# A state space block with a mixture of experts: ScalarE writes D times x into Y's bank and takes small pieces from VectorE

## The reference, cut to what matters

```
xb, z = split(rms_norm(x) @ in_proj_w)
xc    = silu(causal_conv(xb, 4 taps) + conv_b)
dt, B, C = split(xc @ x_proj_w);  dt = softplus(dt * dt_proj_w + dt_proj_b)
h_t   = exp(dt_t * A) * h_{t-1} + dt_t * B_t * xc_t      # per channel and state
y_t   = sum_states(h_t * C_t) + D * xc_t
out   = (y * silu(z)) @ out_proj_w + residual
```

## Time and profile before

| | |
|---|---|
| median of 3 runs | 2586.57 us (2585.44 to 2588.78) |
| profiled execution, its own time | 2586.42 us |
| its span in the trace | 2584.6 us |
| VectorE busy | 2375.5 us |
| TensorE busy | 2365.7 us |
| ScalarE busy | 1607.1 us |
| a steady pass (norms of pass 6 to norms of pass 7) | 967.91 to 1117.45: 149.5 us |

### The profile page before, as it was taken

The page is one execution under the profiler, slowest core; times in us unless marked ns, Lnnn a source line. Parts: engine busy times, 40 slices in busy tenths (PEclk is TensorE's granted clock), DMA queues, the critical chain, the costliest instruction groups (busy, mean ns, idle before and its releaser), DMA issues.

```text
span 2584.6 us, 26581 instructions
## 1 busy us (share of the span) xinstructions
PE 2365.7 (92%) x8416; PEld 1172.9 (45%) x8416; DVE 2375.5 (92%) x2821; ACT 1607.1 (62%) x3202; POOL 1495.0 (58%) x531
## 2 busy tenths in 40 slices
PE   5556899999999999999999999999999999988988
PEld 2112354544545454454545445454545545443554
DVE  3999999999999999999999999999999999999542
ACT  6566567675766666675766667666666756654231
POOL 0554566657565665666566666656666566666421
PEclk9768899999999999999999999999999999999999
DMA  4441433535353453535354353524444452543231
GB/s 154 163 147 69 144 130 124 177 98 186 113 160 120 139 168 103 180 117 166 110 157 150 104 179 118 184 95 156 149 126 159 122 183 84 166 133 96 72 76 57
DMA packets 172759, 344.48 MB, mean 133 GB/s; under 512 B 16043, under 2 KB 81356, under 8 KB 164172
## 3 DMA queue, kind: packets, MB, share of 16 engines
q1 hardware_dynamic: 164700, 334.93, 38.5%
q0 software_dynamic: 7920, 7.87, 2.3%
HBM read 291.35 MB, written 51.38 MB: 133 GB/s over the span
## 4 chain that ended last, share of the span: by engine, by line
DVE 63%; issue 18%; PE 10%; ACT 8%; DMA 1%; POOL 0%; DVEq 0%; SPq 0%; ACTq 0%; POOLq 0%
DVE hs L1051 29%; DVE hs L1037 14%; DVE th L1151 5%; DVE th L1146 5%; PE MY L503 2%; PE Gp L485 2%; PE Up L493 2%; DVE XC L1004 2%; ACT dA L592 1%; ACT SZ L665 1%; DVE SZ L1058 1%; ACT L592 1%; DVE DX L1026 1%; ACT L665 1%; PE FP L410 1%
## 5 line engine op out<-in xcount | busy, mean ns | idle before, releaser
L924 POOL TENSOR_TENSOR hs<-hs,Cb 128x2048 f32<-128x2048 f32 x256 | 1159.8, 4531 | 163.6 <-DVE hs L1037 163.6
L592 ACT ACTIVATE dA<-dtr,A 128x512 f32<-128x512 f32 x1024 | 700.7, 689 | 734.5 <-DVE hs L1051 732.2
L909 POOL TENSOR_TENSOR th<-th,cmb 128x512 f32<-128x512 f32 x256 | 326.3, 1278 | 906.2 <-DVE hs L1037 804.5
L1051 DVE TENSOR_TENSOR_SCAN hs<-dA,carry,hs 128x512 f32<-128x512 f32 x512 | 627.2, 1265 | 5.9 <-ACT dA L592 5.5
L1051 DVE TENSOR_TENSOR_SCAN hs<-dA,hs 128x512 f32<-128x512 f32 x512 | 595.3, 1204 | 14.9 <-ACT dA L592 14.4
L1037 DVE TENSOR_TENSOR hs<-dxr,Bb 128x2048 f32<-128x2048 f32 x256 | 588.7, 2300 | 6.9 <-DMA dxr<-dx_d 5.1
L485 PE MATMUL Gp<-x2T,Wgu 128*128 128x512 f32 x1024 | 510.0, 621 | 27.7 <-DVE th L1146 26.8
L503 PE MATMUL MY<-Wdn,th 128*128 128x256 f32 x2048 | 485.8, 381 | 2.0 <-POOL th L909 2.0
L493 PE MATMUL Up<-x2T,Wgu 128*128 128x512 f32 x1024 | 482.7, 594 | 0.0
L503 PEld LDWEIGHTS MY<-Wdn,th 128*128 128x128 f32 x2048 | 383.3, 190 | 138.2 <-issue 92.5
L485 PEld LDWEIGHTS Gp<-x2T,Wgu 128*128 128x128 f32 x1024 | 176.6, 191 | 356.5 <-issue 275.4
(11 more groups left out here) (171 smaller groups left out, 1758.7 us busy)
## 6 DMA issues: line engine op xcount, KB each, us to landing
dxr<-dx_d SPq DMA_DIRECT2D x128, 512.0 KB, 7.2
dtr<-dt_d SPq DMA_DIRECT2D x64, 1024.0 KB, 5.5
cmb<-cm_d SPq DMA_DIRECT2D x256, 256.0 KB, 3.6
Wdn<-in_w_dn SPq DMA_DIRECT2D x256, 128.0 KB, 3.5
Bb<-bc_d SPq DMA_DIRECT2D x64, 256.0 KB, 3.0
Cb<-bc_d SPq DMA_DIRECT2D x64, 256.0 KB, 3.5
dt_d<-XB SPq DMA_DIRECT2D x15, 1024.0 KB, 4.3
dx_d<-DX SPq DMA_DIRECT2D x15, 1024.0 KB, 5.8
```

Source lines behind the costliest of these rows:

```text
L592: act.activation(dA[h % 2][:, :], dtr[:, M % 2, beta, :], ACT.Exp, scale=A[:, k:k + 1]).then_inc(s_dA, 1)
L909: pool.tensor_tensor(th[:, q % NTH, :], th[:, q % NTH, :], cmb[:, q % 2, :], ALU.mult).then_inc(m_a, 1)
L924: pool.tensor_tensor(hs[:, G % NH, :, :], hs[:, G % NH, :, :], Cb[:, s, :].unsqueeze(1).broadcast_to([P, NBETA, CH]), ALU.mult).then_inc(s ...
L1051: dve.tensor_tensor_scan(hv, dA[h % 2][:, :], hv, first, ALU.mult, ALU.add).then_inc(s_h, 1)
```

## The change

ScalarE writes D times x into Y's bank (`y_begin`), with D as the scale per partition, as soon as `y_out` has read the bank: in the second lot of groups 1, 5 and 13 right behind keep_ends, and in group 9 behind softplus. TensorE waits for it (`y_seed`), adds the states onto it without a starting product, and Ddiag is gone. A product at the start marks the bank's elements once (`y_first`).

For this Y must have the natural order of channels. The stores of dt and dx now permute: each is four transfers of 32 partitions instead of one of 128, in the start too. The host no longer permutes weights.

The variances of all norms (a multiplication and an addition on 4 to 12 numbers per partition) and the product `comb` of the routing go from VectorE to ScalarE.

ScalarE's pieces move: `e_squares` from the second to the first lot of group 3; `z_squares` from the first lot of group 3 to the first lot of group 15 of the pass before; `e_xT` to the second lot of group 12 and the first lot of group 13; `f_silu_z` from group 12 to group 13, behind `y_begin`. TensorE's turns move to the end of group 12 and to group 13 behind the expert's up.

```
-        def channels(t, c):
-            return t.rearrange('(c m p) t -> c p m t', m=MT, p=P)[c]
+        def channels(t, c, b):
+            return t.rearrange('(c m k b) t -> c b k m t', m=MT, k=CB, b=NBETA)[c, b]
...
                     if g == 10:
                         sp.wait_ge(f_act.sem, f_act.at(c, 'dt'))
-                        sp.dma_start(channels(dt_d, c), dt).then_inc(st_dt, 16)
+                        for b in range(NBETA):
+                            sp.dma_start(channels(dt_d, c, b), dt[b * CB:(b + 1) * CB, :, :]).then_inc(st_dt, 16)
...
                 if s == 0:
-                    if G > 0:
-                        pe.wait_ge(y_gate, G // NSIG)
-                    pe.wait_ge(f_act.sem, f_act.at(c, 'silu_x'))
-                    if G == 0:
-                        pe.wait_ge(w_dve, 2)
-                    pe.matmul(Y[:, :], Ddiag[:, m, :], XC[:, c % 2, m, :], start=True, stop=False)
+                    pe.wait_ge(y_seed, G // NSIG + 1)
...
                 if in_e(p) and g == 13:
-                    e_turn(p, 0)
+                    e_turn(p, 1)
...
-                if in_e(p) and g == 13:
-                    e_turn(p, 1)
+                if in_e(p) and g == 12:
+                    e_turn(p, 0)
...
+            def variance(v, sq):
+                return act.activation(v, sq, ACT.Copy, scale=1.0 / DM, bias=LN_EPS)
...
+            def y_begin(M):
+                c, m = divmod(M, MT)
+                act.wait_ge(f_act.sem, f_act.at(c, 'silu_x'))
+                if M > 0:
+                    act.wait_ge(y_gate, M)
+                else:
+                    act.wait_ge(y_first, 1)
+                act.activation(Y[:, :], XC[:, c % 2, m, :], ACT.Identity, scale=d_col[:, m:m + 1]).then_inc(y_seed, 1)
...
+            def p_comb(p):
+                c = p - 1
+                act.wait_ge(p_dve.sem, p_dve.at(c, 'wr'))
+                if c > 0:
+                    act.wait_ge(fp_full, filled(p - 1, 'ct'))
+                for b in range(TB):
+                    ins = act.activation(comb[:, b * NE:(b + 1) * NE], picked[:, b, 0:NE], ACT.Copy, scale=R[:, 7, 2 * TB + b:2 * TB + b + 1])
+                ins.then_inc(p_act.sem, 1)
...
-                if in_e(p) and g == 14:
+                if in_e(p) and g == 13:
                     e_xT(p, 1)
-                if g == 3 and 0 <= p - 3 < NC - 2:
-                    z_squares(p - 3)
+                if 0 <= p + 2 < NC and g == 3:
+                    e_squares(p + 2)
+                if g == 15 and 0 <= p - 2 < NC - 2:
+                    z_squares(p - 2)
...
+                if g in (1, 5, 13) and 0 <= G - 1 < NGRP:
+                    y_begin((G - 1) // NSIG)
...
-                if F and g == 12:
+                if in_e(p) and g == 12:
+                    e_xT(p, 0)
+                if F and g == 13:
                     f_silu_z(p)
-                if in_e(p) and g == 13:
-                    e_xT(p, 0)
```

More of the change, by code:

```diff
@@ L179, in sandwich_kernel @@
         banks = [FP, Gp, Up, MY[0], MY[1]]
[L181 to L184, removed]
+        n_dve = Steps(sem('n_dve'), rsqrt_names('r') + ['nb'])
+        e_act = Steps(sem('e_act'), ['sum', 'nm', 'sq', 'var', 'xr'])
+        f_act = Steps(sem('f_act'), ['xT0', 'xT1', 'raw0', 'tap0', 'raw1', 'tap1', 'raw2', 'tap2', 'raw3', 'tap3', 'z0', 'silu_x', 'xd', 'dt', 'z1', 'z2', 'z3'],
+            ['xT0', 'xT1', 'raw0', 'tap0', 'raw1', 'tap1', 'raw2', 'raw3', 'tap2', 'tap3', 'silu_x', 'z0', 'xd', 'dt', 'z1', 'z2', 'z3'])
+        s_gate = sem('s_gate')
         f_dve = Steps(sem('f_dve'), [f'c{k}{m}' for m in DVE_CONV for k in range(HIST)] + ['hist', 'dx'])
@@ L295, in first_part @@
                 sp.wait_ge(dt_0, 1)
-                sp.dma_start(channels(dt_d, 0)[:, 0, :], dt[:, 0, :]).then_inc(st_dt0, 16)
+                for b in range(NBETA):
+                    sp.dma_start(channels(dt_d, 0, b)[:, 0, :], dt[b * CB:(b + 1) * CB, 0, :]).then_inc(st_dt0, 16)
                 sp.wait_ge(dx_0, 1)
-                sp.dma_start(channels(dx_d, 0)[:, 0, :], DX[:, 0, :]).then_inc(st_dx0, 16)
+                for b in range(NBETA):
+                    sp.dma_start(channels(dx_d, 0, b)[:, 0, :], DX[b * CB:(b + 1) * CB, 0, :]).then_inc(st_dx0, 16)
                 load_B(0, 0)
@@ L307, in first_part @@
                 sp.wait_ge(ld_dt[0], 16)
-                sp.dma_start(channels(dt_d, 0)[:, 1:, :], dt[:, 1:, :]).then_inc(st_dt, 16)
+                for b in range(NBETA):
+                    sp.dma_start(channels(dt_d, 0, b)[:, 1:, :], dt[b * CB:(b + 1) * CB, 1:, :]).then_inc(st_dt, 16)
                 sp.wait_ge(f_dve.sem, f_dve.at(0, 'dx'))
-                sp.dma_start(channels(dx_d, 0)[:, 1:, :], DX[:, 1:, :]).then_inc(st_dx, 16)
+                for b in range(NBETA):
+                    sp.dma_start(channels(dx_d, 0, b)[:, 1:, :], DX[b * CB:(b + 1) * CB, 1:, :]).then_inc(st_dx, 16)
                 load_B(0, 2)
@@ L532, in first_part @@
                     f_in(-1, f'z{m}')
+                pe.matmul(Y[:, :], ident, Win[:, 0, 0:CH], start=True, stop=True).then_inc(y_first, 1)
                 e_turn(-1, 0)
@@ L620, in e_squares @@
                 squares(xin, n_sq[:, 0:TB], n_nm[:, c % 4, TB:2 * TB], dx_half).then_inc(e_act.sem, 1)
+                act.wait_ge(e_act.sem, e_act.at(c, 'sq'))
+                act.activation(n_v[:, 0:TB], n_sq[:, 0:TB], ACT.Copy, scale=(1.0 + RMS_EPS) / DM, bias=LN_EPS * RMS_EPS)
+                variance(n_v[:, TB:2 * TB], n_sq[:, 0:TB]).then_inc(e_act.sem, 1)
             def e_norm(c):
@@ L715, in p_squares @@
                     ins.then_inc(p_act.sem, 1)
+                    act.wait_ge(p_act.sem, p_act.at(c, 'sq'))
+                    variance(n_v[:, 2 * TB:3 * TB], n_sq[:, TB:2 * TB]).then_inc(p_act.sem, 1)
             def p_squares2(p):
@@ L719, in p_squares2 @@
                 squares(x1[:, (p - 1) % 2, :, :], b_s, n_nm[:, (p - 1) % 4, TB:2 * TB], dx_half).then_inc(p_act.sem, 1)
+                act.wait_ge(p_act.sem, p_act.at(p - 1, 'sq2'))
+                variance(p_w[:, 0, :], b_s[:, :]).then_inc(p_act.sem, 1)
             def p_ro(p):
@@ L752, in p_cmT @@
                     act.wait_ge(st_cm, 16 * (p - 1))
-                act.activation(cmT[:, :], FP[0:NE, :], ACT.Copy).then_inc(p_act.sem, 1)
+                act.activation(cmT[:, :], FP[0:NE, :], ACT.Copy, scale=0.5).then_inc(p_act.sem, 1)
             def z_my(c):
@@ L775, in z_squares @@
                 squares(my, sq, nm, waste).then_inc(z_act.sem, 1)
+                act.wait_ge(z_act.sem, z_act.at(c, 'sq'))
+                variance(v, sq).then_inc(z_act.sem, 1)
             def z_norm(c):
@@ L867, in _ @@
                     e_sums(p + 2)
-                if 0 <= p + 2 < NC and g == 3:
-                    e_squares(p + 2)
                 if R_ and g == 3:
@@ L887, in _ @@
                     f_softplus(p)
+                if R_ and g == 9:
+                    p_comb(p)
+                if g == 9 and 0 <= G - 1 < NGRP:
+                    y_begin((G - 1) // NSIG)
                 if R_ and g == 10:
@@ L943, in prepare @@
                 ins.then_inc(w_dve, 1)
-                for m in range(MT):
-                    dve.tensor_scalar(Ddiag[:, m, :], to_y, d_col[:, m:m + 1], None, ALU.mult)
                 for m in PE_CONV:
@@ L973, in newton @@
                 done('y1')
-            def variance(v, sq):
-                return dve.tensor_scalar(v, sq, 1.0 / DM, LN_EPS, ALU.mult, ALU.add)
             def norms(p):
```

86 lines of the change are left out of this document (36 added, 50 removed).

## The result

| | before | after |
|---|---|---|
| median | 2586.01 us (2581.38 to 2588.78, 6 runs) | 2604.00 us (2600.15 to 2606.28, 6 runs) |
| profiled execution, its own time | 2586.42 us | 2606.28 us |
| its span | 2584.6 us | 2604.5 us |
| a steady pass, mean of an even and an odd one | 149.87 us | 151.37 us |

The ratio is 1.0071, with a 95% interval from 1.0061 to 1.0081: slower, by 18 us in the medians and 19.9 us in the profiled executions. The forecast was 2608.5 us. A pass's time here is half the distance from the norms of pass 5 to those of pass 7.

What follows compares the result with a forecast made beforehand. VectorE was taken as the bound, by its own work or its waits; -9.0 + 1.3 - 2 + 0.5 + 20 + 8.7 + 2 + 0.5 = +22.0 on 2586.42 us gave 2608.5 us, range 2575 to 2622.

Steps and rivals of the forecast that it cites:

- The two pieces off VectorE: Combine product and second norm's variance leave VectorE in each pass: 0.56 x 16 = 9.0 us less.
- The norms gain nothing: In group 4 VectorE already waits for ScalarE's squares; the variance on ScalarE adds +0.08 x 16 = +1.3 us.
- Group 13: Late xT1, then seed and SiLU, make scan 2 of group 14 wait 2.4 us (odd 2.0): +20 us.
- z_squares: In group 15, without the convolution's cover, it makes group 0's gate late by 0.67 us in 13 passes: +8.7 us.
- The start: Six more store issues of 0.33 us on SP, ahead of the first product's loads: +2 us.
- The D products off TensorE: TensorE loses 64 products, which hold VectorE up only in the last pass and at the start: -2 us.
- The seed in group 5: In even passes seed and a variance take 0.94 us against 0.9 us of room: +0.5 us in all.
- B: Rival: xT1's turn is ready when ScalarE gets to it, main term 2 not 20; 2590.5 us, chance 0.12.
- C: Rival: ScalarE's new order has room, z_squares hides, group 4's squares come before VectorE asks; 2571.5 us, chance 0.16.
- D: Rival: the seed surfaces also in groups 1, 5 and 9, about 0.3 us each; 2622.5 us, chance 0.10.

Runs made afterwards that it cites:

- kernel 6: The changed kernel with the routing's product `comb` and the second norm's variance back on VectorE: 2612.71 us.
- kernel 9: The kernel before with only `comb` and the second norm's variance moved to ScalarE: 2578.75 us.
- kernel 3: The changed kernel with the SiLU back in group 12 and turns and xT back in groups 13 and 14; the seeds stay: 2588.32 us.
- kernel 1: The changed kernel with z's SiLU back in group 12, ahead of xT0: 2592.29 us.
- kernel 7: The changed kernel with each seed written twice, one write behind the other: 2613.19 us.
- kernel 10: The changed kernel with the SiLU, turns, xT, z_squares and e_squares back where they were before: 2581.79 us.
- kernel 11: The kernel before with each store of dt and dx issued as four of 32 partitions, in the old layout: 2588.16 us.
- 12: The kernel before with `comb` and the second variance on ScalarE, and z's SiLU in group 2 of the next pass: 2565.93 us.
- kernel 5: The changed kernel with VectorE's norms of group 4 behind its product for the next group (`inputs`): 2681.90 us.
- kernel 2: The changed kernel with turns and xT back in groups 13 and 14, the SiLU left in group 13 ahead of xT0: 2627.99 us.

## Why the prediction was right

The forecast's direction and mechanism held, and the sum was 2 us too high against the profiled execution, 4.5 against the median. Term by term:

- **The two pieces off VectorE, -9.0.** Right: +8.7 when put back (kernel 6), -7.6 when done alone (kernel 9).
- **The norms gain nothing, +1.3.** Right in kind, too small in size. The wait went from 0.60 to 0.92 us in an odd pass, from 0.57 to 1.04 in an even one; the variance instruction that lay inside it (0.20 us) went. Net +0.12 and +0.27 a pass, about +3 in all, by the trace.
- **Group 13, +20.** The waits, 2.38 and 1.97 us, are the forecast's 2.4 and 2.0. Summed over all passes of the trace, less the waits in group 13 that went, they are 17.8 us (passes 0, 1 and 14 add little, and odd passes 7 and 13 wait 2.16). Taking the placement back gave 15.7 by the medians and some 20 by the traces (kernel 3). The cause as put, xT1's write waiting 2 us for its turn and the SiLU behind it, stands in the trace, and kernel 1 shows that the SiLU's place decides. A second seed there adds 0.7 us to the wait (kernel 7).
- **z_squares, +8.7.** The mechanism was right, the size too large. The gate waited 0.40 us, not 0.67: from the start of decay 3 (1079.09) to the gate there are 4.91 us instead of the 5.09 that I had summed, and VectorE's own way from there to the gate was 4.51 instead of 4.43. In 13 passes 0.40 us are 5.2. Undone beside the other moves it gave 6.5 us by the medians and 5 by the traces (kernel 10 against kernel 3).
- **The start, +2.** The term was worked out with too cheap an issue (0.33 for 0.43 to 0.46 us) and came out as 3.9 us at the first product (53.98 against 50.06), yet alone it costs 1.9 us by the medians, with an interval from -0.5 to +3.9, and 0.9 by the spans (kernel 11). It came out near the 2 us by luck, because two errors cancel: the issue was priced too low, and I did not ask whether a later wait would take the delay back.
- **The D products off TensorE, -2.** Not isolated, and no run shows a gain. VectorE's two waits for Y in pass 2 are gone in the changed kernel, but they went in kernel 11 too, which keeps the products. What can be said is that the seed and all that comes with it gained nothing: kernel 10 stands 3.0 us behind kernel 9. The forecast also left out what becomes of TensorE with the seed. Between the norms of pass 2 and those of pass 13, read in stretches of 2 us, its granted clock falls below 1.00 in 11 places in the changed kernel and in 2 in the kernel before; in every kernel here with the seed there are 11 or more, in kernels 9, 11 and 12, without it, at most 3.
- **The seed in group 5, +0.5.** No wait there. Doubled, with 0.7 us more of ScalarE's time, it showed 0.15 us (kernel 7), so one seed left some 0.55 us of room, an estimate, where I had counted none.

Not foreseen was a wait of 0.40 us in group 9 of passes 3, 5, 9 and 11, 1.6 us in all: x2T's second half waited 1.55 us for TensorE's turn, and e_norm and two decays lay behind it.

```profile
866.33 0.60 ACT L761 ACTIVATE x2T<-FP 128x512 f32<-128x512 f32 x1 [1.55 <-PE FP L464]
```

That turn belongs to TensorE's group 8, and TensorE's clock had fallen in its group 7. The expert's gate in group 7 of pass 5, which has the wait in group 9, and of pass 7, which has not:

```profile
849.92 2.63 PE L491 MATMUL Gp<-x2T,Wgu 128*128 128x512 f32 x4 [2.55 <-DVE th L1169]
852.34 2.97 PE L499 MATMUL Up<-x2T,Wgu 128*128 128x512 f32 x4
```

```profile
1152.65 1.98 PE L491 MATMUL Gp<-x2T,Wgu 128*128 128x512 f32 x4 [2.54 <-DVE th L1169]
1154.47 1.94 PE L499 MATMUL Up<-x2T,Wgu 128*128 128x512 f32 x4
```

TensorE had waited the same time in both. In pass 5 the granted clock was then 0.78 and 0.50 (850 to 854), and gate and up took 1.7 us more; in pass 7 it stayed at 1.00. The four passes with the wait are the four whose clock fell in group 7; why it fell in these and not in passes 7 and 13, no row shows.

Of the rivals, B (the turn is in time) fell to the 2.02 us in front of xT's write. C asked for the squares of group 4 to end earlier; they did not, and kernel 5 showed that avoiding that wait in the other way costs far more. D fell because in the steady passes no decay behind a seed of groups 1, 5 and 9 is late. A balance of the steady pass closes: waits +1.39 (group 13), +0.40 (group 0), +0.39 (norms), +0.20 (group 9, pass 5 of the two) are 2.38; VectorE's instructions gone are 0.56 and 0.20 in the norms' wait, 0.76 or a little more. That leaves about 1.6 a pass where 151.37 - 149.87 = 1.50 are measured. Over the whole run, -8.7, about +3, +17.8, +5.2 and +1.6 make some 19 of the 19.9 us; the rest, the start among it, I have not assigned.

## What to carry to other kernels

When the bounding engine is locked to a helper by a chain of short deadlines, price a moved piece by the list that it lands in: what stands behind it until the next deadline, and what cover (here a convolution of 2.3 us) the bounding engine has in that group. The 4.5 us of table loads and SiLU cost 0.8 us a pass in group 12, about 2 in group 13, and 0.25 us in every second pass in group 2 of the next. Before a single-buffered bank's reader is put behind something long, look at the engine that must refill the bank, and at its clock, since a stall of that engine can cost more than its own length; and before a delay in the start is added to the sum, look for a wait further on that will take it back.

## What the hardware did that I had not expected

- Small VectorE instructions with two inputs in SBUF can be held for the whole of a GpSimd one: 128x16 steps of 0.17 us took 1.26 and 4.44 us beside GpSimd's products, and the kernel took 78 us more (kernel 5).
- A stall cost TensorE its clock: after 3.90 us without work the granted clock was 0.50 from 1075.2 to 1080, and a gate of 1.98 us took 3.30 (kernel 2). After a wait of 2.55 us it fell in pass 5 of the changed kernel, after one of 2.54 us in pass 7 it did not.
- An issue of a quarter store on SP took 0.43 to 0.46 us, against the 0.33 that I had read from the row of a full store, so four pieces cost 1.72 and 1.84 us of the queue.
- Hardly anything stood between a table load and its neighbours: the seed ended at 1065.84, the load ran from 1065.85 for 1.28 us, and the SiLU began at 1067.15.
